# Where the biases of the routed tiles are added: TensorE or VectorE

## The reference

```python
x = x + tanh(g_xattn) * attention(layernorm(x), ctx, ctx)
z = layernorm(x)
shared = swiglu(z @ sw1 + sb1) @ sw2 + sb2
probs = softmax(z @ gate_w + gate_b)          # top 2 of 8 experts, cw = their probabilities
out_e = swiglu(z @ rw1[e] + rb1[e]) @ rw2[e] + rb2[e]
x = x + tanh(g_ffn) * (shared + sum_e cw[e] * out_e)
```

## Time and profile before

| | us |
|---|---|
| median of 3 runs | 777.78 (774.02 to 780.13) |
| the profiled execution, in all | 784.94 |
| its span | 783.1 |
| PE, DVE, ACT, POOL busy in it | 675.2, 504.0, 431.1, 238.7 |

### The profile page before, as it was taken

The page is one execution under the profiler, slowest core; times in us unless marked ns, Lnnn a source line. Parts: engine busy times, 40 slices in busy tenths (PEclk is TensorE's granted clock), DMA queues, the critical chain, the costliest instruction groups (busy, mean ns, idle before and its releaser), DMA issues. The chain is left out here.

```text
span 783.1 us, 12572 instructions
## 1 busy us (share of the span) xinstructions
PE 675.2 (86%) x3568; PEld 340.3 (43%) x3568; DVE 504.0 (64%) x840; ACT 431.1 (55%) x850; POOL 238.7 (30%) x238
## 2 busy tenths in 40 slices
PE   4787769699999999999999997986487699999970
PEld 3675532133333333333333333534366477777750
DVE  5899888488888888888888884557157332332320
ACT  3665236477777777777777776552133243443430
POOL 8442241331244332230021022006613024434431
PEclk9998888899999999999999999899589899999995
DMA  8799759367777879774566101003982424545434
GB/s 262 269 252 371 136 195 182 71 96 135 177 186 167 178 155 204 187 161 69 78 94 95 35 8 55 7 1 119 390 352 99 148 45 79 90 74 89 65 39 123
DMA packets 84389, 108.39 MB, mean 138 GB/s; under 512 B 18029, under 2 KB 66196, under 8 KB 83383
## 3 DMA queue, kind: packets, MB, share of 16 engines
q1 hardware_dynamic: 72826, 69.05, 40.2%
q0 software_dynamic: 10512, 27.79, 13.6%
q10 hardware_dynamic: 1008, 11.01, 3.5%
HBM read 62.63 MB, written 47.10 MB: 140 GB/s over the span
## 5 line engine op out<-in xcount | busy, mean ns | idle before, releaser
L794 ACT ACTIVATE pr<-psS 128x512 f32<-128x512 f32 x488 | 266.7, 595 | 108.6 <-PE psS L1422 108.5
L1073 DVE TENSOR_REDUCE mneg<-psM 128x1 f32<-128x1024 f32 x240 | 282.6, 1220 | 68.1 <-PE psM L1404 68.0
L1422 PE MATMUL psS<-qst,kst 99*128 99x512 bf16 x488 | 154.2, 389 | 11.3 <-DMA qst<-msb 10.7
L1449 PE MATMUL psO<-pr,vt 128*32 128x512 f32 x1024 | 138.6, 614 | 0.0
L1404 PE MATMUL psM<-kst,qst 96*128 96x512 bf16 x480 | 127.8, 387 | 6.4 <-DVE mneg L1073 4.1
L1422 PEld LDWEIGHTS psS<-qst,kst 99*128 99x128 bf16 x488 | 40.0, 97 | 159.8 <-ACT pr L794 129.9
L704 POOL DMA_INDIRECT acc<-ysb,zg x39 | 60.2, 1543 | 103.1 <-DMA acc<-ysb,zg 60.2
L1293 DVE TENSOR_TENSOR rg<-psH,rs 128x256 f32<-128x256 f32 x39 | 16.6, 425 | 92.1 <-ACT rs L921 82.5
L1404 PEld LDWEIGHTS psM<-kst,qst 96*128 96x128 bf16 x480 | 46.3, 98 | 65.7 <-DVE mneg L1073 10.7
L557 POOL TENSOR_TENSOR msb<-mcp,none 16x128 bf16<-16x128 f32 x16 | 6.3, 391 | 209.1 <-ACT mcp L771 209.1
L1665 PE MATMUL psH<-wall,zgT 128*128 x234 | 66.3, 419 | 0.0
(11 more groups left out here) (218 smaller groups left out, 876.8 us busy)
## 6 DMA issues: line engine op xcount, KB each, us to landing
kst<-k_parts SPq DMA_DIRECT2D x96, 128.0 KB, 5.9
w_parts<-wraw POOLq DMA_DIRECT2D x14, 768.0 KB, 4.8
wall<-w_parts ACTq DMA_DIRECT2D x7, 1536.0 KB
v_pad<-vst SPq DMA_DIRECT2D x16, 512.0 KB, 7.6
vt<-v_pad SPq DMA_DIRECT2D x16, 512.0 KB, 7.8
wraw<-wexp POOLq DMA_DIRECT2D x9, 768.0 KB, 6.1
k_parts<-parts SPq DMA_DIRECT2D x16, 384.0 KB, 5.6
qst<-q_parts SPq DMA_DIRECT2D x96, 64.0 KB, 5.4
```

Source lines behind the costliest of these rows:

```text
L794: nc.scalar.activation(pr[:, slot, j], score_bank(s, j), ACT.Exp, scale=SCALE).then_inc(e_done, 1)
L1073: V.tensor_reduce(mneg[:, parity, i:i + 1], psM[:, i % 2], X_AXIS, ALU.max, negate=True).then_inc(m_free, 1)
L1422: mm(score_bank(s, j), kst[:, slot, j, kt * P:(kt + 1) * P], qst[:, slot, j], start=True, stop=True).then_inc(s_full, 1)
L1449: last = mm(psO[j * VW:(j + 1) * VW, u % 2], vt[:, u, k, j * VW:(j + 1) * VW], pr[:, k % 4, j], start=(k == 0), stop=(k == KT - 1), skip_g ...
```

## The change

The two bias products per tile go. The biases lie in SBUF as float32 rows that are the same in all 128 partitions: `b1_bc` (128 x 9 x 512) and `b2_bc` (128 x 9 x 256), loaded by SP with a stride of zero over the partitions, `b2_bc` from the input and `b1_bc` from `b1_rows`, the turned bias, stored once in DRAM. They lie where `a_in`, `zT0`, `zT2` and `zx012` were, so SP loads them only when the last batch's slots are known, six first products of the shared expert are done and three batches are scattered; the base stores of batches 0 and 1 follow behind them. VectorE adds b1 to psR into `hb` (new, `tile_bias`), ScalarE's silu and VectorE's gate read `hb` instead of psR; ScalarE writes the weighted product into `yw` instead of `ysb`, and VectorE adds weight times b2 to it into `ysb` (new, `tile_sum`, in pass i for tile i-3). TensorE's first product waits for `hb_ok` instead of the gate. GpSimd makes no bfloat16 parts, and before the early weights waits for the store of `b1_rows`.

```diff
@@ -77,8 +77,7 @@
-    b1_parts = dram("b1_parts", [3, NE * 4 * P], BF16)
-    b2_parts = dram("b2_parts", [3, NE * D], BF16)
+    b1_rows = dram("b1_rows", [NE * 4, P], F32)
@@ -95,10 +94,7 @@
-        b2_r = sb("b2_r", [NE, D], F32, sP)
-        b2_p = sb("b2_p", [NE, 3, D], BF16, sP)
-        b1_p = sb("b1_p", [NE * 4, 3, P], BF16, sP)
@@ -139,10 +135,12 @@
-        brow1 = sb("brow1", [3, NE, 2 * D], BF16, sZ)
-        brow2 = sb("brow2", [3, NE, D], BF16, sZ)
-        sb("shift", [P, (4 * QT * D + 4 * 2 * DT * BLK + 4 * DT * D + 4 * DT * BLK - 2 * NE * 3 * D) // 4], F32, sZ)
+        b2_bc = sb("b2_bc", [P, NE, D], F32, sZ)
+        hb = sb("hb", [P, 2, 2 * D], F32, sZ)
+        yw = sb("yw", [P, 2, D], F32, sZ)
+        sb("shift", [P, QT * D + 2 * DT * BLK + DT * D + DT * BLK + 2 * DT * BLK + 8 - (NE + YB + 6) * D], F32, sZ)
+        b1_bc = sb("b1_bc", [P, NE, 2 * D], F32, sZ)
...
@@ -347,7 +344,6 @@
-            sp.dma_start(b2_r[:], b2).then_inc(b_in, 16)
@@ -445,10 +441,8 @@
-            sp.wait_ge(bp_ok, 2)
-            for s in range(3):
-                sp.dma_start(b1_parts[s].rearrange("(q p) -> q p", p=P), b1_p[:, s]).then_inc(bp_st, 16)
-                sp.dma_start(b2_parts[s].rearrange("(e d) -> e d", d=D), b2_p[:, s]).then_inc(bp_st, 16)
+            sp.wait_ge(bt_ok, 1)
+            sp.dma_start(b1_rows, b1_t[:]).then_inc(bp_st, 16)
@@ -485,13 +479,15 @@
-            sp.wait_ge(wo_full, NB)
-            sp.wait_ge(h_full, 2)
-            sp.wait_ge(bp_st, 16 * 6)
-            b1_rows = b1_parts.rearrange("s (e c) -> s e c", e=NE)
-            sp.dma_start(brow1[:, 0:NR], b1_rows[:, 1:NE]).then_inc(brow_ld, 16)
-            sp.dma_start(brow1[:, NR:NE], b1_rows[:, 0:1]).then_inc(brow_ld, 16)
-            sp.dma_start(brow2[:], b2_parts.rearrange("s (e c) -> s e c", e=NE)).then_inc(brow_ld, 16)
+            sp.wait_ge(h_full, 6)
+            sp.wait_ge(sl_ok, NB)
+            sp.wait_ge(sc_done, 16 * 2 * QT * (NB - 1))
+            sp.wait_ge(bp_st, 16)
+            sp.dma_start(b2_bc[:], b2.unsqueeze(0).to_broadcast([P, NE, D])).then_inc(brow_ld, 16)
+            b1_flat = b1_rows.rearrange("q p -> (q p)")
+            sp.dma_start(b1_bc[:, 0:NR].rearrange("p e c -> p (e c)"),
+                         b1_flat[4 * P:].unsqueeze(0).to_broadcast([P, NR * 4 * P])).then_inc(brow_ld, 16)
+            sp.dma_start(b1_bc[:, NR], b1_flat[0:4 * P].unsqueeze(0).to_broadcast([P, 4 * P])).then_inc(brow_ld, 16)
@@ -501,7 +497,7 @@
-            sp.wait_ge(sc_done, 16 * 2 * QT * NB)
+            sp.wait_ge(sc_last, 16 * 2 * QT)
@@ -586,17 +582,6 @@
-            pool.wait_ge(bt_ok, 1)
-            pool.wait_ge(b_in, 32)
-            for n, (raw, part) in enumerate(((b1_t, b1_p), (b2_r, b2_p))):
-                nc.gpsimd.tensor_copy(part[:, 0], raw[:]).then_inc(bp_c, 1)
-                pool.wait_ge(bp_c, 3 * n + 1)
-                nc.gpsimd.tensor_tensor(raw[:], raw[:], part[:, 0], ALU.subtract).then_inc(bp_c, 1)
-                pool.wait_ge(bp_c, 3 * n + 2)
-                nc.gpsimd.tensor_copy(part[:, 1], raw[:]).then_inc(bp_c, 1)
-                pool.wait_ge(bp_c, 3 * n + 3)
-                nc.gpsimd.tensor_tensor(part[:, 2], raw[:], part[:, 1], ALU.subtract).then_inc(bp_ok, 1)
-            pool.wait_ge(bp_ok, 2)
@@ -619,6 +604,8 @@
+            pool.wait_ge(bp_st, 16)
+
@@ -667,7 +654,7 @@
                             out_offset=bass.IndirectOffsetOnAxis(ap=slot_u[:, b, k * QT + t:k * QT + t + 1], axis=0),
-                            in_=zx(b)[:, t], in_offset=None, bounds_check=SLOTS - 1).then_inc(sc_done, 16)
+                            in_=zx(b)[:, t], in_offset=None, bounds_check=SLOTS - 1).then_inc(sc_done if b < NB - 1 else sc_last, 16)
@@ -914,11 +900,11 @@
             def tile_silu(i):
-                act.wait_ge(rh_full, i + 1)
+                act.wait_ge(hb_ok, i + 1)
                 if i >= 2:
                     act.wait_ge(rg_ok, i - 1)
-                nc.scalar.activation(rs[:, i % 2], psR[:, i % 2, 0:D], ACT.Silu).then_inc(rs_ok, 1)
+                nc.scalar.activation(rs[:, i % 2], hb[:, i % 2, 0:D], ACT.Silu).then_inc(rs_ok, 1)
@@ -927,11 +913,11 @@
                 e, = table(mybir.EngineType.Activation, T_E + i, 1, NE - 1)
                 act.wait_ge(ry_full, i + 1)
-                if i >= YB:
-
-                    act.wait_ge(issued, DRAIN * ((i - DRAIN) // DRAIN) + 1)
-                nc.scalar.activation(ysb[:, i % YB], psQ[:, i % 2, 0:D], ACT.Identity,
-                                     scale=zg[:, i % ZG, bass.ds(e + D, 1)]).then_inc(ry_ok, 1)
+                if i >= 2:
+
+                    act.wait_ge(ry_ok, i - 1)
+                nc.scalar.activation(yw[:, i % 2], psQ[:, i % 2, 0:D], ACT.Identity,
+                                     scale=zg[:, i % ZG, bass.ds(e + D, 1)]).then_inc(yw_ok, 1)
             act.wait_ge(tab_ok, 2)
@@ -1290,22 +1276,57 @@
             def tile_gate(i):
                 dve.wait_ge(rs_ok, i + 1)
-                V.tensor_tensor(rg[:, i % 2], psR[:, i % 2, D:2 * D], rs[:, i % 2], ALU.mult).then_inc(rg_ok, 1)
+                if i >= 2:
+
+                    dve.wait_ge(rt_full, i - 1)
+                V.tensor_tensor(rg[:, i % 2], hb[:, i % 2, D:2 * D], rs[:, i % 2], ALU.mult).then_inc(rg_ok, 1)
+
+            tile_e = {}
+
+            def tile_load(i, n):
+                tile_e.update(zip(range(i, i + n), table(mybir.EngineType.DVE, T_E + i, n, NE - 1)))
+
+            def tile_bias(i):
+                dve.wait_ge(rh_full, i + 1)
+                if i >= 2:
+
+                    dve.wait_ge(rs_ok, i - 1)
+                    dve.wait_ge(rg_ok, i - 1)
+                V.tensor_tensor(hb[:, i % 2], psR[:, i % 2], b1_bc[:, bass.ds(tile_e[i], 1)].rearrange("p a c -> p (a c)"),
+                                ALU.add).then_inc(hb_ok, 1)
+
+            def tile_sum(i):
+                dve.wait_ge(yw_ok, i + 1)
+                if i >= YB:
+
+                    dve.wait_ge(issued, DRAIN * ((i - DRAIN) // DRAIN) + 1)
+                V.scalar_tensor_tensor(out=ysb[:, i % YB], in0=b2_bc[:, bass.ds(tile_e[i], 1)].rearrange("p a c -> p (a c)"),
+                                       scalar=zg[:, i % ZG, bass.ds(tile_e[i] + D, 1)], in1=yw[:, i % 2],
+                                       op0=ALU.mult, op1=ALU.add).then_inc(ry_ok, 1)
             def tile_g_low(i):
                 dve.wait_ge(rt_hi, i + 1)
                 V.tensor_tensor(gT[:, i % 2, 1], psG[:, i % 2, 0:D].rearrange("p (k t) -> p k t", k=DT),
                                 gT[:, i % 2, 0].bitcast(F32), ALU.subtract).then_inc(rt_ok, 1)
+            dve.wait_ge(tab_ok, 3)
+            tile_load(0, 8)
             tile_low(0)
             tile_low(1)
-            for i in range(TILES_R + 1):
+            dve.wait_ge(brow_ld, 48)
+            for i in range(TILES_R + 3):
+                if i < TILES_R:
+                    tile_bias(i)
+                if i + 2 < TILES_R:
+                    tile_low(i + 2)
                 if i < TILES_R:
                     tile_gate(i)
-                if i + 2 < TILES_R:
-                    tile_low(i + 2)
-                if i:
+                if 0 <= i - 1 < TILES_R:
                     tile_g_low(i - 1)
+                if i >= 3:
+                    tile_sum(i - 3)
+                if i % 4 == 3 and i + 5 < TILES_R:
+                    tile_load(i + 5, 4)
         @block.tensor
@@ -1389,7 +1410,7 @@
-            pe.wait_ge(b_in, 32)
+            pe.wait_ge(b_in, 16)
@@ -1654,17 +1675,16 @@
             def tile_first(i):
-                w, e = tile_regs[i]
+                w = tile_regs[i]
                 pe.wait_ge(zz_ok, i + 1)
-                    pe.wait_ge(rg_ok, i - 1)
-                mm(psR[:, i % 2], ones3[:], brow1[:, bass.ds(e, 1)].rearrange("s a c -> s (a c)"), start=True, stop=False)
+                    pe.wait_ge(hb_ok, i - 1)
                 for n, (zp, wp) in enumerate(((0, 0), (0, 1), (1, 0))):
                                   wall[:, bass.ds(w + (12 * wp + 4 * k), 4)].rearrange("p a c -> p (a c)"),
-                                  start=False, stop=(n == 2 and k == DT - 1))
+                                  start=(n == 0 and k == 0), stop=(n == 2 and k == DT - 1))
                 last.then_inc(rh_full, 1)
@@ -1677,34 +1697,30 @@
             def tile_second(i):
-                w, e = tile_regs[i]
+                w = tile_regs[i]
                 pe.wait_ge(rt_ok, i + 1)
-                    pe.wait_ge(ry_ok, i - 1)
-                mm(psQ[:, i % 2, 0:D], ones3[:], brow2[:, bass.ds(e, 1)].rearrange("s a c -> s (a c)"), start=True, stop=False)
+                    pe.wait_ge(yw_ok, i - 1)
                 for n, (gp, wp) in enumerate(((0, 0), (0, 1), (1, 0))):
                                   wall[:, bass.ds(w + (12 * wp + 8 + 2 * k), 2)].rearrange("p a c -> p (a c)"),
-                                  start=False, stop=(n == 2 and k == DT - 1))
```

(16 more changed lines are left out.)

## The result

| | runs | median us | lowest to highest |
|---|---|---|---|
| before | 4 | 778.54 | 774.02 to 780.13 |
| changed | 4 | 788.37 | 786.92 to 789.72 |

The medians lie 9.8 us apart; the ratio taken over the runs is 1.0141, 95% interval 1.011 to 1.0172: the change makes the kernel slower, by 1.3 to 1.4%. A second series on one chip gave 789.23 (6 runs) against 780.47 (17 runs), ratio 1.0116 (1.0082 to 1.015), which is 9.1 us of 780.47. That series is the measure for the experiments.

A forecast was written before the change was run, and what follows sets the result against it. GpSimd's serial scatter-adds were taken to bound the routed stage, with TensorE almost as long beside them. Terms 3.2 - 1.0 + 5.6 + 0.3 = +8.1 us, carried over to the runs' median of 777.78, gave 786 us, range 774 to 799.

The forecast's parts named there:

- The bound: Routed stage: GpSimd's 39 scatter-adds, 3.57 us per tile, set the end; TensorE's chain, 3.47, runs beside them.
- Ready well before the last add: End of the routed stage: TensorE's chain delivers its last result well before GpSimd's last add.
- First result: Start of the routed stage: the sum at the end of VectorE's fourth pass delays the first add and the end, +3.2 us.
- Read-ahead: Tile loads let in by adds: the longer way to a tile's add starves TensorE, about five gaps, +5.6 us.
- the 33rd add: GpSimd's adds: TensorE's gain removes the wait for a late result at this add, -1.0 us.
- Attention: Before the attention: GpSimd newly waits for the store of the turned bias, one place behind `bo` in SP's queue, +0.3 us.
- Loads: SP and DMA between router and stage: larger bias loads covered by 8.5 us of slack before the first tile's use, zero.
- late-loads rival: Broadcast loads run at half rate or stand before the first tiles: +3 to +5 us on top, 790 us; chance 0.11.
- Passes: Time per routed tile: TensorE 2.95 us (3.47 less 0.52), VectorE 2.82, or 2.9 to 3.1 with register work.
- TensorE sets the end: Rival: TensorE's chain bounds the routed stage, so its saving shows: -17 us, 761 us; chance 0.10.
- the adds alone: Rival: only the later first add counts, gaps stay short and the clock stays up: +2.5 us, 780 us; chance 0.27.
- Mutual blocking: Rival: VectorE operations with two SBUF inputs and GpSimd's adds hold each other up: 16 to 18 us, 795 to 804; chance 0.06.

The follow-up runs named there:

- no_products: Kernel before without its two bias products per routed tile on TensorE and nothing in their place, routed biases missing from the result: 774.25 us, ratio 0.9914.
- before_drain6: Kernel before with only every sixth add waiting for earlier ones to land (12 result buffers) and token indices in their own buffer: 784.81 us, ratio 0.9999.
- sum_sooner: Changed kernel with the sum of tile i - 2, not i - 3, in VectorE's pass i: 779.23 us, ratio 0.9989 to the kernel before.
- index_apart: Changed kernel with token indices also in their own buffer, so a tile's buffer comes free with its sum: 787.35 us, ratio 1.0011 to the kernel before.

## Why the prediction was right

The forecast was 786 us in a range of 774 to 799, the measurement 788.37. By its own steps:

**The bound.** That the adds' chain, and not TensorE's, set the end of the stage is borne out: 20 us less work on TensorE brought 6.7 us (no_products). "Ready well before the last add" was too strong. TensorE's chain was level with it: before_drain6 relieved the adds and gained nothing.

**First result, +3.2.** Measured +3.5 (14.3 against 10.8); sum_sooner took 2.8 of it back.

**Read-ahead, +5.6, and the 33rd add, -1.0.** The adds grew by 4.0 us in this profile and by 2.6 in the next one of the same kernel, against 4.6 together. The mechanism is the forecast one: the 12th tile is waited for first (6.5 us, forecast some 5) and the 15th next, and the granted clock falls behind the gap. There are eight gaps behind the first tile's and not about five. The -1.0 did not come: the 33rd add still waited 0.99 us and the 32nd, punctual before, 3.79. index_apart showed the starved read-ahead as a cause. That one sum a pass earlier would undo first result and starvation together was in the argument (it counts three passes to the sum) but I didn't draw it, so my expectation for sum_sooner was three times too small.

**Attention, +0.3.** Zero. GpSimd's first work behind the new wait starts 0.19 us after the step ahead of it (147.37 to 147.56). Its wait for `bo` ended at 146.70 in place of 144.64, but everything ahead had already been 2 us later in that execution.

**Loads, 0.** The weakest term. The cover named, the 8.5 us between the first tile load and its use, did not hold in this profile: the load went out 6.2 us later after the slots and TensorE waited 4.0 us for it. The misjudged size is the fills, 12.66 us in place of 7.84, issued among 3.5 MB of broadcast and 1 MB of base stores. What it cost, 0 to 2.7 us, is part of the late-loads rival.

**Passes.** TensorE's was forecast at 2.95 from 3.47 less 0.52; VectorE's loop at 2.82, 2.9 to 3.1 with register work. Measured were 2.83, set by VectorE's loop: the register work cost nothing visible. TensorE alone can go at 2.54 (no_products), so its term was mis-sized: the two bias products take 0.93 us of its pass and not 0.52, which is 36 us of work over 39 tiles in place of 20.3. Why that is more than the products' shares of the chain stays open. It made no difference to the forecast, since the adds hid it.

**The rivals.** "TensorE sets the end" (761) and "the adds alone" (780) fell with the second series too. Mutual blocking exists, as the last section shows, but it is small: the adds are 1558 ns in the mean against 1543, 0.6 us in all where 16 to 18 were priced. Of 9 to 10 us, about 3.5 are the first result, 2.6 to 4.0 the starved read-ahead with that 0.6 in it, and 0 to 2.7 the loads; the rest, from nothing to some 4 us, can't be placed, since the profile of before is one execution and its pieces differ between executions by as much. That 788.37 lies so near 786 is therefore in part luck: the loads, put at nothing, and the -1.0 that did not come stand against gaps that cost less than forecast.

## What to carry to other kernels

Work taken off the engine with the longest chain of waits pays only if the chain beside it is shorter by as much; find that out by relieving each of the two in turn, since each edit alone may show little (6.7 and 0 us here) while both together show 18 us. Where buffers are freed by the end of a pipeline, count the passes from the release to the same buffer's next use: a consumer moved one pass back cost 3 us once and another 5 through loads that came late. And an engine shown as busy all the time may still wait inside a loop over two other engines; exchanging two steps of a third engine's order settled it.
